# Gated cross-attention and quantised feed-forward on one core: a transpose DMA in two halves, and a reordering of TensorE and VectorE work around it

## What is computed

```python
x = x + tanh(g_xattn) * xattn(layernorm(x), ctx, mask, ...)   # 16 heads of 32, then Wo, bias, scale, layernorm, gamma, beta
x = x + tanh(g_ffn) * ffn(layernorm(x), ...)

def bit_linear(x, w, b):
    gamma_x = clip(max(abs(x), axis=-1), 1e-5)        # one scale per token
    x_dq = clip(round(x * 127 / gamma_x), -128, 127) * gamma_x / 127
    gamma_w = clip(mean(abs(w)), 1e-5)                # one scale per matrix
    w_dq = clip(round(w / gamma_w), -1, 1) * gamma_w  # ternary weights
    return x_dq @ w_dq.T + b

ffn = bit_linear(silu(bit_linear(x, gate)) * bit_linear(x, val), out)   # hidden width 2048
```

## Time and profile before

| | us |
|---|---|
| median of 3 runs | 797.77 (796.95 to 798.64) |
| time of the profiled run | 797.77 |
| its span, first to last instruction | 795.9 |
| PE busy | 702.9 (88%) |
| DVE busy | 627.8 (79%) |
| ACT busy | 531.9 (67%) |
| POOL busy | 315.7 (40%) |
| share of the chain that ended last: PE, DVE, DMA, issue, ACT | 51%, 21%, 12%, 7%, 7% |

### The profile page before, as it was taken

One profiled execution on the slowest core, in us unless ns is written; L12 is line 12 of the kernel. 1 busy time (PEld: TensorE's weight loads), 2 busy tenths in 40 slices (PEclk: granted clock), 3 DMA queues, 4 the chain that ended last, 5 costly groups with the idle time before them and its releaser, 6 DMA issues.

```text
span 795.9 us, 13407 instructions
## 1 busy us (share of the span) xinstructions
PE 702.9 (88%) x4214; PEld 338.0 (42%) x4214; DVE 627.8 (79%) x1297; ACT 531.9 (67%) x691; POOL 315.7 (40%) x485
## 2 busy tenths in 40 slices
PE   4586755777999999999999999999999999999997
PEld 4342343333544444444444444444444444453443
DVE  6786959489777987798779877987798779778764
ACT  3356867677766875688567856795678557754563
POOL 5100133332464345534543454445544453353430
PEclk9798766999999999999999999999999999999999
DMA  8382375511354336432534264326423552253212
GB/s 290 130 320 83 98 221 126 138 27 41 85 115 109 85 74 126 87 98 59 132 86 92 64 133 98 79 66 132 112 66 79 119 100 53 54 107 90 57 40 66
DMA packets 180189, 82.36 MB, mean 103 GB/s; under 512 B 159269, under 2 KB 159525, under 8 KB 179514
## 3 DMA queue, kind: packets, MB, share of 16 engines
q1 hardware_dynamic: 180154, 81.93, 42.2%
HBM read 39.41 MB, written 10.51 MB: 63 GB/s over the span
## 4 chain that ended last, share of the span: by engine, by line
PE 51%; DVE 21%; DMA 12%; issue 7%; ACT 7%; POOL 1%; SPq 0%; DVEq 0%; POOLq 0%; ACTq 0%
PE psum L1574 18%; PE psum L1565 12%; PE psum L1540 12%; DMA arena<-arena 10%; ACT arena L828 2%; PE psum L1544 2%; DVE psum L1104 1%; PE psum L1601 1%; DVE arena L1109 1%; DVE arena L1042 1%; PE psum L1602 1%; DVE arena L1217 1%; ACT valb_b L742 1%; DVE stats L1059 1%; PE psum L1725 1%
## 5 line engine op out<-in xcount | busy, mean ns | idle before, releaser
L1540 PE MATMUL psum<-ternary,xqT 128*128 128x512 f16 x1024 | 258.6, 379 | 4.1 <-DVE xqT L1134 2.5
L1540 PEld LDWEIGHTS psum<-ternary,xqT 128*128 128x128 f16 x1024 | 97.7, 98 | 122.4 <-issue 4.9
L1565 PE MATMUL psum<-ternary,arena 128*128 128x512 f16 x496 | 123.4, 383 | 14.3 <-DMA arena<-arena 13.8
L610 POOL TENSOR_TENSOR rstd<-var_e,minus_half 128x1 f32<-128x1 f32 x64 | 39.8, 622 | 203.9 <-DVE var_e L1155 113.3
L788 ACT ACTIVATE arena<-psum,dequant 128x512 f32<-128x512 f32 x128 | 86.5, 681 | 48.1 <-PE psum L1544 47.9
L1574 PE MATMUL psum<-wo_hi,arena 128*128 128x512 f16 x256 | 84.0, 390 | 8.3 <-DMA arena<-arena 8.3
L1574 PE MATMUL psum<-arena,wq_hi 128*128 128x512 f16 x256 | 77.5, 385 | 7.0 <-ACT arena L842 7.0
L1117 DVE TENSOR_REDUCE hmax<-arena 128x1 f32<-128x1024 f32 x64 | 77.6, 1213 | 0.8
L1565 PEld LDWEIGHTS psum<-ternary,arena 128*128 128x128 f16 x496 | 46.1, 99 | 71.6 <-issue 14.0
L796 ACT ACTIVATE arena<-arena,round_c,hscale 128x1024 f32<-128x1024 f32 x62 | 73.6, 1237 | 1.7 <-DVE hscale L1129 1.7
L1544 PE MATMUL psum<-bias_parts,inv_rows 128*128 128x512 bf16 x192 | 72.8, 379 | 0.0
(11 more groups left out here) (192 smaller groups left out, 1276.4 us busy)
## 6 DMA issues: line engine op xcount, KB each, us to landing
arena<-in_x SPq DMA_DIRECT2D x64, 256.0 KB, 2.9
out<-arena SPq DMA_DIRECT2D x31, 256.0 KB, 2.8
arena<-in_L_ffn_gate_w SPq DMA_DIRECT2D x4, 1024.0 KB, 10.4
arena<-in_L_ffn_out_w SPq DMA_DIRECT2D x3, 1024.0 KB, 8.0
ternary<-in_L_ffn_val_w SPq DMA_DIRECT2D x2, 1024.0 KB, 10.1
kcur<-k_scratch SPq DMA_DIRECT2D x64, 32.0 KB, 2.2
arena<-arena SPq DMA_TRANSPOSE x75, 4.0
ternary<-in_ctx SPq DMA_DIRECT2D x1, 1024.0 KB, 5.4
```

The source lines that it names most:

```text
L1540: ins = M.matmul(ps[:], xqT[:, t % 2, k, :], w[:, k, cols], start=(k == 0), stop=(k == KC - 1 and not biased))
L1565: ins = M.matmul(psO[:], hidT[t % 2][:, k, :], wo2[:, k, :], start=(k == 0), stop=(k == FC - 1))
```

## The change

1. **The transpose DMA is halved.** `hidden_T` issues two DMA transposes of 1024 columns each, the first once `h16_ready` of the first half is there. `hidT_loaded` counts 32 per tile; both readers, ACT's `hidden_codes` and PE's `down`, wait for both halves.
2. **PE, quarter 3:** 8 chunks of `down`, `xq_transpose`, 8 chunks. **PE, quarter 1 with attention:** `xq_transpose`, `project`, chunks 12 to 15.
3. **DVE, `statistics`:** in quarters 2 and 3 the `x_stats` instructions stand among those for the projection, ahead of `delta`, as in quarters 0 and 1.
4. **DVE, quarter 3:** `new_x` and `x_shift` stand ahead of `hidden(3, 1)` and no longer behind it.
5. **DVE, quarter 1 with attention:** all four `bound` come behind `xq_T`; before, two stood ahead of it.
6. **DVE, `x_shift`:** `scalar_tensor_tensor` in place of `tensor_scalar` with the same operands.

```diff
-        hidT_loaded = per_row("hidT_loaded", 16 * NT)
+        hidT_loaded = per_row("hidT_loaded", 16 * NT * 2)
...
-                wait_alone(sp, s_met_sp, h16_ready, row, 2 * t + 2)
-                sp.dma_start_transpose(hidT[t % 2], hid16).then_inc(hidT_loaded.sem, 16)
+                for h in range(2):
+                    wait_alone(sp, s_met_sp, h16_ready, row, 2 * t + h + 1)
+                    sp.dma_start_transpose(hidT[t % 2][:, h * FC // 2:(h + 1) * FC // 2, :],
+                                           hid16[:, h * F // 2:(h + 1) * F // 2]).then_inc(hidT_loaded.sem, 16)
...
-                V.tensor_scalar(shift1[:, t:t + 1], mv[:, t, 0, 0:1], rstd[:, 0, t:t + 1], -1.0, ALU.mult,
-                                ALU.mult).then_inc(sh1.sem, 1)
+                V.scalar_tensor_tensor(out=shift1[:, t:t + 1], in0=mv[:, t, 0, 0:1], scalar=-1.0,
+                                       in1=rstd[:, 0, t:t + 1], op0=ALU.mult, op1=ALU.mult).then_inc(sh1.sem, 1)
...
-                    pre_last = pre and update and tx >= 2
-                    pre = pre and not pre_last
                     if pre:
                         x_stats_start(c, tx)
...
-                    if pre_last:
-                        x_stats(c, tx)
...
-                        if n == (1 if ffn and t == NT - 1 else 0):
+                        if n == 0:
                             if update:
                                 new_x(*nxt)
                             if pre and not early:
                                 x_shift(c, t)
...
-                    if att and t == 1 and b is not FIRST:
-                        for i in range(NPAIR // 4):
-                            bound(i)
                     if update and att and t < 2:
                         xq_T(*nxt)
...
-                        for i in range(NPAIR // 4, NPAIR // 2):
+                        for i in range(NPAIR // 2):
                             bound(i)
...
-                    before = AFTER_SCORES if att and t == 1 else FC if t == NT - 1 else FC // 2
                     if finish and not (att and t == 1):
-                        down(*last, range(before))
-                    if update:
+                        down(*last, range(FC // 2))
+                    if update and att and t == 1:
+                        xq_transpose(*nxt)
+                    if update and not (att and t == 1):
                         xq_transpose(*nxt)
...
-                    if finish and before < FC:
-                        down(*last, range(before, FC))
                     if att and t == 1 and ffn:
                         wait(pe, p_ready, a, NPAIR)
                         project(*ahead(b, t, 2))
+                    if finish:
+                        down(*last, range(AFTER_SCORES if att and t == 1 else FC // 2, FC))
```

More of the change, by code:

```diff
@@ L823, in hidden_codes @@
                         last, u = ahead(row, t, -1)
-                        wait(act, hidT_loaded, last, 16 * (u + 1))
+                        wait(act, hidT_loaded, last, 16 * 2 * (u + 1))
                     if ffn and not prev and (t, h) == (0, 0):
@@ L1265, in body @@
                                 x_shift(c, t)
-                        if n == 0:
                             if out_w_now and t == 0:
@@ L1562, in down @@
                         wait(pe, ys_ready, last, u + 1)
-                        wait(pe, hidT_loaded, row, 16 * (t + 1))
+                        wait(pe, hidT_loaded, row, 16 * 2 * (t + 1))
                     for k in chunks:
```

## The result

| | before | after |
|---|---|---|
| median, us | 797.36 (795.45 to 798.64) | 805.37 (803.74 to 806.10) |
| time and span of the profiled run | 797.77, 795.9 | 805.14, 803.3 |

The ratio is 1.0100, 95% interval 1.0074 to 1.0126: slower by 8 us, where 3.2 us less were forecast, and above the range's 799.0.

A forecast was written before the change was run, and what follows sets the result against it. PE was taken to set the time of a pass, with DVE or ACT bounding places in quarters 1 and 2. Terms 3.9 - 1.7 + 0.3 - 4.0 - 1.7 = -3.2 gave 794.6 us, range 792.6 to 799.0.

The forecast's parts named there:

- the costing of parts 5 and 6 at nothing: Bounds behind `xq_T`: cost 0, cover 0.7 us; `x_shift` in its new form: 0 +- 0.05 us.
- the four rivals: Clock stays low 796.3 (0.27); halves land late 798.7 (0.10); quarter 2 slower 801.6 (0.13); quarter 3 free 790.7 (0.12).
- half of the excess: Quarter 3, `new_x` at 1.07 us beside 0.75 for a like-sized row: half the excess gone, -0.2 us.
- Pass 7 and the clock: Pass 7: shorter transpose waits, end 4.0 us earlier; last `down` keeping TensorE's upper clock, -1.7 us.
- Quarter 3 of a steady pass: Passes 0 to 5: eight chunks stand behind the wait for ACT and POOL, +0.65 us per pass (+0.35 to +1.05).
- The interleaving: Quarter 3, DVE: `x_stats` among the projection's statistics takes 2.51 us where the other order takes 3.02, -0.5 us.
- the wait of `new_x` for POOL's root: Quarter 3: `new_x`, now right behind `delta`, must wait for POOL's root, about +0.3 us.
- Quarters 1 and 2: Passes 0 to 5: DVE starts `hidden` in quarter 2 sooner, -0.28 us per pass; bounds for six passes 0.6 or -0.5.
- Pass 6: Pass without `x_stats`: quarter 2 +0.6 us as the moved chunks pass through, quarter 3 -0.3, sum +0.3.
- the 1.17 us of DMA wait: Quarter 3, before `down`: PE's wait for the transpose turns into some 1.8 us of waiting for ACT and POOL.

The follow-up runs named there:

- a_no5: Changed kernel with part 5 undone (two of the four bounds ahead of `xq_T` again): 797.64 us against 795.45 for the kernel before, ratio 1.0031.
- b_5: Kernel before with part 5 alone (all four bounds behind `xq_T`): 804.59 us against 796.17, ratio 1.0087.
- a_no56: Changed kernel with parts 5 and 6 undone, so parts 1 to 4 alone: 792.24 us against 795.45 for the kernel before, ratio 0.9955.
- b_13: Kernel before with parts 1 and 3 (halved transpose, `x_stats` ahead of `delta`): 783.43 us against 796.17, ratio 0.9827; run again, 783.70 us, ratio 0.9858.
- b_123: Kernel before with parts 1, 2 and 3 (halved transpose, new order on PE, `x_stats` ahead of `delta`): 792.45 us, ratio 0.9962.
- a_pool_small: Changed kernel, all parts in, with POOL's two adds cut from 512 to 8 columns: 789.60 us against 796.17 for the kernel before, ratio 0.9905.
- a_134: Kernel before with parts 1, 3 and 4 (the last moving `new_x` and `x_shift` ahead of `hidden(3, 1)`): 784.33 us, ratio 0.9867.
- a_no6: Changed kernel with part 6 undone (`x_shift` as `tensor_scalar` again): 799.25 us against 795.45 for the kernel before, ratio 1.0046.

## Why the prediction was wrong

**The step that failed is the costing of parts 5 and 6 at nothing.** Part 5: "two more of 0.65 us each behind `xq_T` end at 447.25. Cost 0, cover 0.7 us". The cover was right, the duration was not. POOL runs two instructions there (L649, then the add of beta), 445.38 to 448.17 in the trace of before, the first of them begun beside the last bound. Part 5 pushes four bounds in a row into them: 4.53 us where 4 x 0.65 = 2.6 was reckoned, 1.93 more. Less the cover of 0.7 that leaves 1.2, and 1.14 (after against a_no5) and 1.10 (b_5 against before) were measured. Part 6: "the nearest row, L1199, takes 0.21, so 0 +- 0.05". The nearest row by shape, but L1199 has one tensor input and stands where POOL is idle. Beside POOL it is +1.02 us, and +1.02 is what the stretch of quarter 3 gained (40.34 against 39.32). Together 2.1 us per pass, six passes, 12.6: -3.2 + 12.6 = +9.4, measured +8.0. None of the four rivals has this mechanism; all of them keep both parts at nothing.

The row that gave it away was used: "`new_x` took 1.07 us, long for its shape beside the 0.75 us of the like-sized L1104". The prediction gave back half of the excess and never asked what it was. Had the POOL timeline been laid beside it, the question "which other DVE instruction moves beside a POOL instruction?" would have led to both parts, and the bound from above of each would have been a POOL instruction, 1.3 to 1.6 us, not 0.05.

**The rest, step by step** (parts 1 to 4, a_no56 against before):

- *Sum:* -3.2 forecast, -3.2 measured (792.24 against 795.45). That it fits so closely is luck: the terms below, as measured, make 1.5 - 1.2 + 1.2 - 5.7 = -4.2 where 3.9 - 1.7 + 0.3 - 5.7 was forecast. Quarter 3 was 2.4 too dear, and pass 6 and quarters 1 and 2 were 1.4 too cheap.
- *Pass 7 and the clock:* -4.0 forecast, with -1.1 for each of three quarters in it, and -1.7 for the clock. Measured -1.05, -1.03 and -3.65 in the stretches, 5.7 in all, as forecast; in the kernel after the landing is 3.0 us, the last wait 1.39 in place of "about 1.6", the clock 1.00. The choice on the clock was nearly even and fell on the right side.
- *Quarter 3 of a steady pass:* mechanism right, size too large: +0.65 forecast, +0.24 measured (39.33 against 39.09). The waits of PE are 0.73 and 0.35 us in the drawing, not 1.3 and 0.5. DVE's chain, from the statistics to the end of `xscale`, is 7.71 us where it was 8.55, so 0.84 shorter and not 0.4. The interleaving was put at -0.5; the wait of `new_x` for POOL's root, put at +0.3, is 0.04 (`delta` ends at 471.99, `new_x` starts at 472.03); and the whole excess of `new_x` is gone (0.75 us), -0.3 and not -0.2.
- *Quarters 1 and 2:* -0.28 forecast, -0.20 measured (18.62 and 22.95 against 18.75 and 23.02), within its bounds. As forecast, `hidden` in quarter 2 waits for PE (L1106, 0.34 us). But b_13 has these 0.2 us without the new order, so the gain is the interleaving's.
- *Pass 6:* +0.6 for quarter 2, +0.70 measured. For quarter 3 -0.3 was forecast and +0.53 measured. DVE and POOL of a_no56 there:

```profile
714.68 1.70 DVE L1169 SCALAR_TENSOR_TENSOR delta<-delta,rstd,arena 128x512 f32<-128x512 f32 x1
...
714.56 1.27 POOL L647 TENSOR_TENSOR arena<-arena 128x512 f32<-128x512 f32 x1
```

  `new_x` reads two tensors from SBUF and now starts 0.12 us behind POOL's add of the output, so it waits out the rest of it: 1.70 us where 0.75 is its own length. This is the cost of part 4, in the one pass where the two start together (b_123, without part 4, takes 13.67 us in that quarter and a_no56 14.57). The wait is the one of part 6 once more, and an experiment shows it: in a_pool_small, where POOL's add is 0.20 us long, this `new_x` takes 0.75 and the quarter 13.63. It also explains a_134's pass 7: `new_x` takes 1.70 us there too (708.05), everything behind it on DVE comes some 0.9 us later against PE, and the first `down` of pass 7 waits 0.92 us for its transpose, where b_13's waits 0.22.
- *What the sum hid:* the four parts gain 3.2 us as +8.75 from part 2 and about -12 from parts 1 and 3 (b_13, -11.2 to -12.7). The prediction took the new order on PE and the halved transpose as one thing, "the 1.17 us of DMA wait are not gained; they turn into some 1.8 us of waiting for ACT and POOL". That holds with part 2. Left in the old order, sixteen chunks go on hiding both, and parts 1 and 3 pay in full.

**Left open.** By the times part 6 costs 0.54% (4.3 us, after against a_no6) and by the stretches 6.2; the two ratios' intervals leave room for both. Why `project` starts 0.4 us later behind a wait at L1555, and what moves 0.2 us in quarter 0, isn't shown. A kernel that keeps the order of part 5 and moves POOL's instructions elsewhere wasn't tried.

## What to carry to other kernels

When an instruction of DVE is moved or changes its form, lay POOL's timeline beside its old and its new place, and take a whole POOL instruction as the upper bound of its price if it has two tensor inputs in SBUF, as `x_shift` and `new_x` here, or is a large `tensor_scalar` from SBUF to SBUF like the bounds (128 x 1024 in 0.65 us; the one of `x_shift`, one element per partition, was not held). A row that is longer than its shape explains is a mechanism at work, and is to be named before anything is costed by it. And test an order on one engine apart from the wait that it is meant to use: here a gain of 11 to 12 us lay in two of six parts, and the other four gave all of it back and more.

## What was not expected of the hardware

- A DVE instruction of one element per partition was held 1.0 us by a POOL instruction of 128 x 512, and ended with it within 0.02 us in two kernels; in another form, `tensor_scalar` with the second operand as a scalar, it took 0.20 us beside POOL.
- The two engines take turns, the later one waiting: four bounds of 0.68, 0.69, 1.66 and 1.75 us, 4.53 in place of 2.6, and POOL's add 1.71 in place of 1.27.
- TensorE's granted clock stayed at 1.00 after a wait of 1.39 us, and averaged 0.72 after one of 2.52 us.
- Two transposes of 128 x 1024, issued 1.24 us each, landed 3.0 us after the issue, one of 128 x 2048 after 4.3.
